# One maximum of 1,024 columns over two neighbouring chunks of attention scores

## What is computed

```python
scores = jnp.einsum('bhqd,bhkd->bhqk', q_full, k_full) * scale
causal = jnp.triu(jnp.ones((s, s), dtype=bool), k=1)
scores = jnp.where(causal, -jnp.inf, scores)
attn = jax.nn.softmax(scores.astype(jnp.float32), axis=-1).astype(q_full.dtype)
out = jnp.einsum('bhqk,bhkd->bhqd', attn, v)
```

## Time and profile before

| | us |
|---|---|
| median of 3 runs | 1697.91 (1697.68 to 1703.39) |
| profiled execution | 1701.13 |
| its span | 1699.4 |
| head loop in it | about 73 to 1227 |

### The profile page before, as it was taken

One profiled execution on the slowest core, in us unless ns is written; L12 is line 12 of the kernel. 1 busy time (PEld: TensorE's weight loads), 2 busy tenths in 40 slices (PEclk: granted clock), 3 DMA queues, 4 the chain that ended last, 5 costly groups with the idle time before them and its releaser, 6 DMA issues. The chain is left out here.

```text
span 1699.4 us, 38029 instructions
## 1 busy us (share of the span) xinstructions
PE 1560.8 (92%) x14452; PEld 1309.5 (77%) x14452; DVE 1182.0 (70%) x2472; ACT 1020.6 (60%) x2009; POOL 306.5 (18%) x752
## 2 busy tenths in 40 slices
PE   6789998999999999999999999999839999989997
PEld 4577787877788788888888888888727877867886
DVE  4567777776777777787787788778655546576564
ACT  3456665765666666677677667667524455545573
POOL 5411111111111211211211121221000002020231
PEclk9889999999999999999999999999969999999999
DMA  7000000000000000000000000000013100000000
GB/s 221 0 1 1 2 2 1 2 2 2 1 2 2 1 2 2 1 2 2 2 2 2 2 2 2 2 2 2 2 41 84 40 1 1 1 29 13 1 26 25
DMA packets 27524, 22.47 MB, mean 13 GB/s; under 512 B 9660, under 2 KB 25148, under 8 KB 27220
## 3 DMA queue, kind: packets, MB, share of 16 engines
q1 hardware_dynamic: 27348, 20.05, 4.1%
HBM read 17.95 MB, written 2.10 MB: 12 GB/s over the span
## 5 line engine op out<-in xcount | busy, mean ns | idle before, releaser
L784 ACT ACTIVATE pT_hi<-pT 128x512 f16<-128x512 f32 (+3 forms) x640 | 341.5, 534 | 302.7 <-PE pT L702 300.1
L905 DVE TENSOR_TENSOR pT_lo<-pT,pT_hi 128x512 f16<-128x512 f32 (+3 forms) x640 | 387.6, 607 | 147.5 <-ACT pT_hi L784 141.3
L773 ACT ACTIVATE pr<-pS,nmx 128x512 f32<-128x512 f32 (+3 forms) x640 | 401.1, 627 | 21.6 <-DVE nmx L896 19.8
L893 DVE TENSOR_REDUCE cmx<-pS 128x1 f32<-128x512 f32 x576 | 339.0, 617 | 65.4 <-PE pS L689 60.9
L702 PE MATMUL pT<-ident,pr 128*128 128x128 f32 x2176 | 348.3, 276 | 16.0 <-DVE pT_lo L905 14.5
L702 PEld LDWEIGHTS pT<-ident,pr 128*128 128x128 f32 x2176 | 253.1, 140 | 54.9 <-ACT pr L773 23.8
L687 PE MATMUL pS<-lT_hi,qT_hi 128*128 128x512 f32 (+2 forms) x640 | 281.5, 440 | 4.2 <-ACT pr L773 2.7
L744 PE MATMUL pO<-c_hi,pT_hi 128*128 128x65 f16 x2176 | 265.7, 194 | 18.4 <-DVE O L923 17.8
L745 PE MATMUL pO<-c_lo,pT_hi 128*128 128x65 f16 x2176 | 266.5, 193 | 0.0
L746 PE MATMUL pO<-c_hi,pT_lo 128*128 128x65 f16 x2176 | 263.7, 192 | 0.0
L1308 PE MATMUL pGU<-lT_hi,W_all 128*128 128x512 f32 (+1 forms) x640 | 221.1, 405 | 16.1 <-ACT sgb L1388 12.1
(11 more groups left out here) (268 smaller groups left out, 2461.5 us busy)
## 6 DMA issues: line engine op xcount, KB each, us to landing
X<-in_x SPq DMA_DIRECT2D x4, 512.0 KB, 6.2
wo<-in_w_o SPq DMA_DIRECT2D x1, 2048.0 KB, 11.1
out<-X SPq DMA_DIRECT2D x8, 256.0 KB, 2.0
raw<-in_wd SPq DMA_DIRECT2D x14, 128.0 KB, 2.2
raw<-in_wg SPq DMA_DIRECT2D x13, 128.0 KB, 2.7
raw<-in_wu SPq DMA_DIRECT2D x13, 128.0 KB, 2.6
wqn<-in_w_qn SPq DMA_DIRECT2D x1, 1536.0 KB, 16.3
raw<-in_qg SPq DMA_DIRECT2D x6, 128.0 KB, 2.5
```

The lines of the kernel that those rows point to most:

```text
L773: act.activation(pr[:, at % RING, 0:n * P], pS[at % 4][:, 0:n * P], ACT.Exp, bias=nmx[:, p % 4:p % 4 + 1]).then_inc(sem("exped"), 1)
L784: act.activation(pT_hi[:, a % 4, 0:chunk[a][2] * P], src, ACT.Copy).then_inc(sem("t_hi"), 1)
L893: ch.inc(dve.tensor_reduce(cmx[:, p % 2, c:c + 1], pS[at % 4][:, 0:n * P], AX.X, ALU.max))
L905: dve.tensor_tensor(pT_lo[:, a % 4, 0:w], src, pT_hi[:, a % 4, 0:w], ALU.subtract).then_inc(sem("t_lo"), 1)
```

## The change

The four banks of scores become two tensors of two banks each, in the same place. Where chunk `at` has an odd number, is not the first of its head and is full (512 columns), the step of the chunk before it takes no maximum, and the step of chunk `at` takes one over both, 1,024 columns. `cmx` then has one column for each maximum and not for each chunk. A head that is left with one maximum needs no second reduction.

```diff
-                pS = [ps(loop, f"pS{b}", [P, BT]) for b in range(4)]
+                pS2 = [ps(loop, f"pS{b}", [P, 2, BT]) for b in range(2)]
+                pS = [pS2[b // 2][:, b % 2, :] for b in range(4)]
...
+                        both = lambda at: at % 2 == 1 and chunk[at][1] > 0 and chunk[at][2] == 4
+
                         def maximum(at):
 
                             p, c, n = chunk[at]
                             n_c = tile_at(p) // 4 + 1
-                            if c == 0 and p >= 4:
+                            if at + 1 < n_chunks and chunk[at + 1][0] == p and both(at + 1):
+                                return
+                            parts_of = [k for k in range(first[p], first[p + 1]) if not (k + 1 < first[p + 1] and both(k + 1))]
+                            k = parts_of.index(at)
+                            if k == 0 and p >= 4:
                                 dve.wait_ge(sem("exped"), first[p - 3])
                             dve.wait_ge(sem("scored"), at + 1)
+                            src, axes = (pS2[at % 4 // 2][:], AX.XY) if both(at) else (pS[at % 4][:, 0:n * P], AX.X)
                             whole_ = nmx[:, p % 4:p % 4 + 1]
-                            if n_c == 1:
-                                dve.tensor_reduce(whole_, pS[at % 4][:, 0:n * P], AX.X, ALU.max, negate=True).then_inc(sem("maximum"), 1)
+                            if len(parts_of) == 1:
+                                dve.tensor_reduce(whole_, src, axes, ALU.max, negate=True).then_inc(sem("maximum"), 1)
                                 return
-                            ch.inc(dve.tensor_reduce(cmx[:, p % 2, c:c + 1], pS[at % 4][:, 0:n * P], AX.X, ALU.max))
-                            if c == n_c - 1:
+                            ch.inc(dve.tensor_reduce(cmx[:, p % 2, k:k + 1], src, axes, ALU.max))
+                            if at == parts_of[-1]:
                                 ch.wait()
-                                dve.tensor_reduce(whole_, cmx[:, p % 2, 0:n_c], AX.X, ALU.max, negate=True).then_inc(sem("maximum"), 1)
+                                dve.tensor_reduce(whole_, cmx[:, p % 2, 0:len(parts_of)], AX.X, ALU.max, negate=True).then_inc(sem("maximum"), 1)
```

## The result

The changed kernel takes 1726.85 us (median of 4 runs, 1724.76 to 1728.48) against 1699.01 for the kernel before in the same session: a ratio of 1.0159, interval 1.0144 to 1.0174. It is 1.6% slower. The profiled execution took 1724.76 us, its span 1723.0.

The account below looks back on a forecast made before the run. PE was taken to bound the loop, DVE having free time but holding PE up. Delays of 14.9 + 3.1 + 1.5 + 6.8 + 1 (first group, last head) = 27.3 us on the 1697.91 median gave 1725.2 us, range 1706 to 1745.

Parts of the forecast that it names:

- The price of the merged maximum: On DVE, a maximum over 1,024 columns in two banks takes 1.21 us, bounded above by 1.28.
- What DVE saves: On DVE, 0.07 us per merged pair, 9.5 us, which buys nothing beyond the delays; busy time falls 10 to 20 us.
- rival A: DVE's saved work counts: 136 mergers and 16 L896 save 12.5 us, giving 1685; chance 0.05.
- Step 1: Tiles 12 to 15, copy of O or another turned tile behind L896: 31 x 0.48 = 14.9 us of PE delay.
- Step 2: Third head of each group of four, tiles 12 to 15, 16 in all: L905 delays the transpose, 3.1 us.
- Step 3: Fourth heads of tiles 12 to 15: projection covers the delay, nothing; three heads feeding xn cost 1.5 us.
- Step 4: Tiles 8 to 11, from 670 us: 13 heads without room cost 5.9 us, 6 with 0.3 of room 0.9 us.
- Tile 7: Merged maximum ends 0.33 us later, but the next transpose comes 1.0 us after L905 ends: no cost.
- B: Later PE gaps shrink because ACT's backlog paces; only about 24 heads without room count, 7 us: 1705; chance 0.12.
- C: Every head with a merged maximum, 104 without tile 7, passes its 0.5 us on: 52 us, 1750; chance 0.08.

Follow-up runs that it names:

- kernel with two late reductions: Changed kernel's order, but each pair's maximum taken as two reductions of 512 columns, not one of 1,024: 1735.44 us, ratio 1.0213 to the kernel before.
- additional reduction in the burst: Kernel before plus one unused 512-column reduction right ahead of L896 in 104 heads of tiles 8 to 15, nothing merged: 1742.46 us, ratio 1.0252.
- additional reduction in the hole: Kernel before plus one unused 512-column reduction right behind the first maximum in the same 104 heads of tiles 8 to 15: 1716.3 us, ratio 1.0104.
- first pairs only: Changed kernel with only the 96 pairs merged that do not end a head: 1727.0 us, ratio 1.0151 to the kernel before.
- the mergers in the order with an earlier chunk between chunks 2 and 3: All 136 mergers, with an earlier chunk worked off between scores of chunks 2 and 3 in four-chunk heads: 1832.36 us; same order unmerged 1819.17.
- that with chunks 0 and 1 side by side: All 136 mergers, four-chunk heads scoring chunks 0 and 1 together, earlier chunk behind both: 1730.88 us, ratio 1.0178; same order unmerged 1710.81.

## Why the prediction was right, point by point

**The forecast** was 1725, 27.3 us above before; the medians are 27.8 apart in the first session. It came from delays of PE that were summed, and these can be checked one by one in the starts of the same matmuls.

**The price of the merged maximum**, 1.21 us, is measured: 1.20 to 1.23. Two banks in one instruction cost what the slope over one bank says.

**What DVE saves** was put too low: 12.5 us in rival A (136 x 0.07 and 16 L896), and its busy time fell by 20.8. The kernel with two late reductions, which has every instruction of before, separates the two causes:

```profile
PE 1574.8 (91%) x14452; PEld 1315.7 (76%) x14452; DVE 1172.6 (67%) x2472; ACT 1026.3 (59%) x2009; POOL 306.7 (18%) x752
```

DVE is busy 9.4 us less there although nothing is merged: a reduction that ran alone (0.68 us) now runs behind another and overlaps it (0.60). The mergers take another 11.4 us, 2.5 for the 16 L896 and 0.07 for each of the 136. None of it was PE's, so the sum did not suffer.

**Step 1**, 31 places at which the copy of O or another turned tile stands behind L896: expected 14.9 us. Measured: 28 first value matmuls, 13.7 us, and 3 transposes, 1.4 us: 15.1. This is two thirds of the loss of the stretch.

**Step 2**, the third heads of tiles 12 to 15: expected 3.1 us, measured 1.3 (1.6 with the first group of heads). The mechanism is right and the size wrong by half. In tile 15 I let L905 start 0.03 us after the end of L896; in the trace it starts 0.07 after the start of L896 (141.56 against 141.49), as the reciprocal in the earlier trace rows already did. So the delay of the transpose is 0.25 and not 0.39.

**Step 3**, the fourth heads: nothing, and 1.5 us for xn. Measured: 0.4 us in all, 0.2 of it xn. The wait for xn before 261.18 grew by 0.21 and the two others by nothing: I take it that the projection, which PE did meanwhile, covered the later exp; no run separates that.

**Step 4**, tiles 8 to 11: expected 6.8 us, measured 7.1 without the wait for O at 673 us, which step 1 has. The sum is right, and the list of heads nearly: 12 heads lose more than 0.35 us and 7 lose 0.1 to 0.35, where I had 13 and 6. The merged last pairs of tile 11, to which I gave 1 to 2 us before the experiment on them, cost nothing.

**Tile 7**: nothing expected, nothing measured.

The steps make 24 us in place of 27.3. The medians are 27.8 us apart, the profiled executions only 23.6: 23.5 in the stretch, 1.3 ahead of the loop, 2.2 behind it and 3.4 less in the first four heads. Differences of the size of the last three appear between kernels that are alike there, too. The 4 us by which the medians are further apart lie in executions that were not profiled, and no trace places them; the profiled execution of the changed kernel is the fastest of its four. That the forecast met the median within 2 us is therefore luck in part; the sum was 3 us high.

**Rivals.** A (saved DVE work counts) is out: DVE saved 20.8 us and the kernel is slower, and tile 7, where DVE saves most for each merger, gained 0.0 us. B (the delay is absorbed) is out: all 28 waits for O grew. C (every head passes it on) did not come true at 0.53 us. The two kernels with 0.60 us more in the burst come closer to its 52 us: the stretch loses 37 and 41 us, 7 and 3 of them by falls of the clock. The prediction had put 3 to 4 us on those 0.07 us; in the medians the kernel with two late reductions lies 34.4 above before and the changed one 27.8, each in its own session, so they cost about 6.6.

## What to carry to other kernels

An instruction that can start early on an engine with free time costs little or nothing; merged with a later one, all its work is done at the later time. Before merging, look at what is queued behind the merged instruction and whether the third engine waits for that. A room hides a delay up to its size, and everything above it is paid in full. So a delay's cost is no straight line: third heads of tile 12 lost nothing by about 0.5 us, while the copies of O passed on nearly all of it.

## What the runs showed of the hardware

**Neighbouring DVE instructions overlap.** In the changed kernel L913 starts at 141.56, 0.09 us before L904 ends (141.49 and 0.16). So a merger saves 0.07 us against two reductions back to back and not a whole fixed part of 0.15.

**TensorE's clock fell inside the loop** after a long wait. Before and in the changed kernel the granted clock is 1.00 from 120 to 1,230 us. In the kernel with two late reductions it fell five times in that time. The first time stands behind this wait:

```profile
131.16 0.19 PE L745 MATMUL pO<-c_hi,pT_hi 128*128 128x65 f16 x1 [1.59 <-DVE O L933]
```

Windows of that kernel around it (stretch, length, busy times, clock):

```profile
122.00:129.00 7.00, 7.00 (x74) 5.92 (x73) 4.22 (x10) 3.12 (x9) 2.63 (x6) 1.00 0.01 4
129.00:132.50 3.50, 1.91 (x25) 1.48 (x23) 2.73 (x8) 2.27 (x6) 0.00 (x0) 1.00 0.00 0
132.50:136.00 3.50, 3.50 (x16) 3.14 (x15) 1.42 (x3) 1.96 (x4) 0.00 (x0) 0.52 0.00 0
```

PE had been busy 1.91 of 3.50 us, with one wait of 1.59 us for O in it; then it ran at half its clock (1.2 and not 2.4 GHz) for about 3.4 us and came back. With the additional reduction in the burst it fell twice, the first time right after PE had waited for the low half of a turned tile:

```profile
290.27 0.63 PE L703 MATMUL pT<-ident,pr 128*128 128x128 f32 x4 [2.08 <-DVE pT_lo L908]
```
```profile
291.20:294.60 3.40, 3.40 (x26) 2.88 (x24) 1.81 (x3) 1.87 (x4) 0.00 (x0) 0.51 0.00 0
```

In the changed kernel PE waited up to 2.0 us in such places and the clock stayed, so the length of the wait alone does not decide it. One fall each also stands in the traces of the additional reduction in the hole (436 us, after a wait of 1.86), of the first pairs only (440 us, 1.87), of the mergers in the order with an earlier chunk between chunks 2 and 3 (221 us) and in that with chunks 0 and 1 side by side (740 us, 1.59). The changed kernel waited 1.86 us at 439 us, too, without one. A fall costs 1.3 to 1.7 us by the same matmuls at either level (about 2 in the one at 221 us), so five of them are some 7 of the 14 us that the profiled execution of two late reductions lies above the changed kernel in the stretch.

The first four heads owe much of their scatter to the same thing. In the profiled execution of before the clock was at half from 94.3 to 101.1 us, and in that of the changed kernel it was not. The first window is of before, the second of after:

```profile
94.30:101.10 6.80, 6.19 (x23) 4.83 (x23) 3.26 (x7) 2.56 (x5) 0.00 (x0) 0.50 0.00 0
```
```profile
94.30:101.10 6.80, 5.48 (x51) 4.55 (x52) 4.66 (x7) 4.54 (x9) 0.00 (x0) 1.00 0.00 0
```

It does not take the change for that: in the kernel with mergers in tile 7 only, whose first four heads have the instructions of before, the clock was not at half there either, and these heads took 40.9 us and not 43.3 (39.9 in the changed kernel). How often either kernel has that fall is left open.
